# Bucket ranks of the third layer: running totals on VectorE from whole-group counts, in stages

## The reference

```python
Wh = h @ W + b
row, col = (edge_index[0], edge_index[1])
Wr, Wc = Wh[row], Wh[col]
dot = jnp.sum(Wr * Wc, axis=-1)
nr = jnp.sqrt(jnp.sum(Wr * Wr, axis=-1))
nc = jnp.sqrt(jnp.sum(Wc * Wc, axis=-1))
sim = dot / jnp.maximum(nr * nc, EPS)
prop_pos = segment_sum((base * relu(sim))[:, None] * Wc, row, num_segments=n_nodes)
prop_neg = segment_sum((base * -relu(-sim))[:, None] * Wc, row, num_segments=n_nodes)
return scale * (coeff[0] * prop_pos + coeff[1] * prop_neg + coeff[2] * Wh)
```

## Time and profile before

| | |
|---|---|
| median of 3 runs | 9442.85 us (9428.52 to 9460.71) |
| the profiled execution | 9496.65 us, its span 9494.9 us |
| PE busy over the span | 5779.2 us (61%) |
| POOL busy | 5102.6 us (54%) |
| DVE busy | 4579.2 us (48%) |
| ACT busy | 3305.8 us (35%) |
| TensorE's granted clock, mean | 0.748 |

### The profile page before, as it was taken

The page is one execution under the profiler, slowest core; times in us unless marked ns, Lnnn a source line. Parts: engine busy times, 40 slices in busy tenths (PEclk is TensorE's granted clock), DMA queues, the critical chain, the costliest instruction groups (busy, mean ns, idle before and its releaser), DMA issues. The chain is left out here.

```text
span 9494.9 us, 103424 instructions
## 1 busy us (share of the span) xinstructions
PE 5779.2 (61%) x22770; PEld 3507.7 (37%) x22771; DVE 4579.2 (48%) x10542; ACT 3305.8 (35%) x6399; POOL 5102.6 (54%) x5308
## 2 busy tenths in 40 slices
PE   0068788888840777777777524444443444499997
PEld 0034343434320333333333222222222222299997
DVE  2545555555542333333333353444444444477777
ACT  0023333333320333333333311111111111299997
POOL 5666666666656666666666555566655656500000
PEclk9978887878765777777777755555555555599998
DMA  8233333333321333333333211111111111122221
GB/s 325 80 93 111 109 107 110 109 110 106 112 62 49 98 98 103 102 103 103 106 103 104 81 30 55 52 52 53 52 51 51 53 51 53 47 59 59 60 59 52
DMA packets 566846, 800.69 MB, mean 84 GB/s; under 512 B 163210, under 2 KB 307466, under 8 KB 566506
## 3 DMA queue, kind: packets, MB, share of 16 engines
q1 hardware_dynamic: 371944, 482.15, 16.8%
q0 software_dynamic: 172640, 195.75, 9.3%
q10 hardware_dynamic: 22178, 121.99, 3.2%
HBM read 497.93 MB, written 301.41 MB: 84 GB/s over the span
## 5 line engine op out<-in xcount | busy, mean ns | idle before, releaser
L696 POOL DMA_INDIRECT rows_by_src_bucket<-arena,put_idx x1568 | 1532.8, 978 | 1019.2 <-DVE arena L1342 549.3
L625 POOL DMA_INDIRECT G<-h_rows,src_idx x1568 | 1483.2, 946 | 852.7 <-issue 456.2
L625 POOL DMA_INDIRECT G<-in_x,src_idx x1470 | 1395.7, 949 | 808.5 <-issue 432.2
L1172 DVE TENSOR_TENSOR_SCAN xd_t<-same,xd_t,ps_two 128x512 f32<-128x512 bf16 x588 | 749.1, 1274 | 1044.1 <-remote 870.0
L746 PE MATMUL ps_gv<-attr,w_attr 65*128 65x512 f32 x1568 | 1104.1, 842 | 220.4 <-issue 126.3
L749 PE MATMUL ps_gv<-arena,w_src 128*128 128x512 f32 x1568 | 1044.3, 803 | 0.0
L728 PE MATMUL ps_two<-ident,inj 128*128 128x128 f32 x2352 | 445.1, 322 | 938.1 <-DMA inj<-first_edge_rows 648.2
L928 ACT COPY arena<-ps_out 128x512 f32<-128x512 f32 x392 | 230.5, 588 | 2124.7 <-remote 1864.0
L813 PE MATMUL ps_pos<-arena 128*128 128x392 f32 x390 | 316.3, 914 | 1017.1 <-DVE arena L1195 621.9
L1234 DVE TENSOR_SCALAR arena<-ps_gv 128x512 f32<-128x512 f32 x392 | 266.5, 680 | 1228.5 <-remote 607.4
L752 PE MATMUL ps_gv<-xd_t,w_dst 128*128 128x512 f32 x1568 | 773.8, 616 | 3.5 <-issue 3.5
(11 more groups left out here) (226 smaller groups left out, 10251.1 us busy)
## 6 DMA issues: line engine op xcount, KB each, us to landing
inj<-first_edge_rows SPq DMA_DIRECT2D x588, 256.0 KB
running_sums<-arena SPq DMA_DIRECT2D x392, 256.0 KB
same<-same_dst SPq DMA_DIRECT2D x1176, 64.0 KB
rows_by_src_bucket<-zeros ACTq DMA_DIRECT2D x98, 703.5 KB
first_edge_rows<-zeros ACTq DMA_DIRECT2D x56, 896.0 KB
attr<-in_attr_t SPq DMA_DIRECT2D x392, 128.0 KB
G<-h_rows,src_idx POOLq DMA_INDIRECT x1568
rows_by_src_bucket<-arena,put_idx POOLq DMA_INDIRECT x1568
```

The costliest lines, as they stand in the source:

```text
L625: pool.indirect_dma_start(out_, None, table_in, bass.IndirectOffsetOnAxis(ap=index, axis=0)).then_inc(s, 16)
L696: pool.indirect_dma_start(bucket_d, bass.IndirectOffsetOnAxis(ap=put_idx[:, buf, k:k + 1], axis=0), put[:, buf, k], None).then_inc(s_added ...
L1172: v.tensor_tensor_scan(xd_t[:, buf % 2], same[:, buf], ps_inj, xd_t[:, 1 - buf % 2, COLS - 1:COLS], ALU.mult, ALU.add).then_inc(s_scan, 1)
```

## The change

A group's running count no longer passes through the ranks. PE counts the whole group at once (`count_group`: `ones_b` as weights, both halves summed into one of two new buffers `ps_counts`), and DVE adds that to `reached` (`add_counts`), of which there are now 4 buffers. `rank` takes both halves of a group from the same `reached`; the second half gets the marks of the first by one more matmul with `ones_b`. The ranks have two buffers in PSUM (`ps_ranks`), `hot` has 4, `sq` has 2. ACT copies no ranks: only `fill_put` is left. All stages are now written by `pipeline` with lags: on DVE marks 0, carry 1, add 1, place 2; on PE turn and count 0, turn back 1, ranks 1.

```diff
-        hot = tile(2, SLOTS * NT // 2).rearrange("p b c -> p (b c)").bitcast(BF16).rearrange("p (b c) -> p b c", b=2)
+        hot = tile(NB, SLOTS * NT // 2).rearrange("p b c -> p (b c)").bitcast(BF16).rearrange("p (b c) -> p b c", b=NB)
-        reached = tile(2, CB)
-        sq = tile(SLOTS * D)
+        reached = tile(NB, CB)
+        sq = tile(2, SLOTS * D)
+        ps_ranks = ((ps_pos, ps_out), (ps_gv[:, 1, 0], ps_gv[:, 1, 1]))
+        ps_counts = (ps_gv[:, 0, 0], ps_gv[:, 0, 1])
...
-            def place(h, buf):
-                def rank(k):
...
-                turn_inj(2, h, buf)
-                pe.wait_ge(s_hot, done(1, h, buf))
-                rank(0).then_inc(s_below[0], 1)
-                pe.wait_ge(s_scan, done(2, h, buf))
-                pe.wait_ge(s_sq, done(0, h, buf, 1))
-                for j in range(TILES):
-                    mm = pe.transpose(ps_g[:, j * P:(j + 1) * P], turned(xd_t[:, buf % 2], j), ident[:])
-                mm.then_inc(s_wt, 1)
-                rank(1).then_inc(s_below[1], 1)
-            pipeline(pe, (place, 0))
+            def turn_first(h, buf):
+                turn_inj(2, h, buf)
+            def count_group(h, buf):
+                pe.wait_ge(s_hot, done(1, h, buf))
+                pe.wait_ge(s_reached, done(0, h, buf, 1))
+                for k in range(2):
+                    mm = pe.matmul(ps_counts[buf % 2][:, 0:CB], ones_b[:], hot[:, buf, k * CB:(k + 1) * CB],
+                                   start=k == 0, stop=k == 1)
+                mm.then_inc(s_counted, 1)
+            def turn_back(h, buf):
+                pe.wait_ge(s_scan, done(2, h, buf))
+                pe.wait_ge(s_sq, done(0, h, buf, 1))
+                for j in range(TILES):
+                    mm = pe.transpose(ps_g[:, j * P:(j + 1) * P], turned(xd_t[:, buf % 2], j), ident[:])
+                mm.then_inc(s_wt, 1)
+            def rank(h, buf):
+                if at_start(h) and buf == 0:
+                    pe.wait_ge(s_halves, 2)
+                pe.wait_ge(s_reached, done(0, h, buf))
+                for k in range(2):
+                    pe.wait_ge(s_ranked[k], done(0, h, buf, 2))
+                    to = ps_ranks[buf % 2][k][:, 0:CB]
+                    pe.matmul(to, last_row, reached[:, buf], start=True, stop=False)
+                    if k:
+                        pe.matmul(to, ones_b[:], hot[:, buf, 0:CB], start=False, stop=False)
+                    pe.matmul(to, upto[:], hot[:, buf, k * CB:(k + 1) * CB], start=False,
+                              stop=True).then_inc(s_below[k], 1)
+            pipeline(pe, (turn_first, 0), (count_group, 0), (turn_back, 1), (rank, 1))
...
-            def copy_ranks(h, buf):
-                for k, ranks_now in enumerate((ps_pos, ps_out)):
-                    act.wait_ge(s_below[k], done(0, h, buf))
-                    nc.scalar.copy(reached[:, k], ranks_now[:, 0:CB]).then_inc(s_reached[k], 1)
-                    if k == 0:
-                        fill_put(h, buf)
...
-                act.wait_ge(s_norm, done(0, h, buf, 1))
-                nc.scalar.activation(sq, ps_g, ACT.Square).then_inc(s_sq, 1)
+                act.wait_ge(s_norm, done(0, h, buf, 2))
+                nc.scalar.activation(sq[:, buf % 2], ps_g, ACT.Square).then_inc(s_sq, 1)
...
-            pipeline(act, (copy_ranks, 0))
+            pipeline(act, (fill_put, 0))
...
+            def mark_group(h, buf):
+                mark_buckets(1, h, buf)
+            def carry_group(h, buf):
+                carry_dst(2, h, buf)
+            def add_counts(h, buf):
+                dve.wait_ge(s_counted, done(1, h, buf))
+                dve.wait_ge(s_reached, done(0, h, buf))
+                dve.wait_ge(s_below[1], done(0, h, buf, NB - 1))
+                v.tensor_tensor(reached[:, (buf + 1) % NB], reached[:, buf], ps_counts[buf % 2][:, 0:CB],
+                                ALU.add).then_inc(s_reached, 1)
+            def place_group(h, buf):
+                for k in range(2):
+                    dve.wait_ge(s_below[k], done(0, h, buf))
+                    v.tensor_tensor(ranks[:, k], ps_ranks[buf % 2][k][:, 0:CB], hot[:, buf, k * CB:(k + 1) * CB],
+                                    ALU.mult).then_inc(s_ranked[k], 1)
+                    dve.wait_ge(s_ranked[k], done(0, h, buf))
+                    then(v.tensor_reduce(pos[:, k * CLASSES:(k + 1) * CLASSES],
+                                         ranks[:, k].rearrange("p (c t) -> p c t", t=NT), AX.X, ALU.add))
+                put_free(dve, h, buf)
+                v.tensor_scalar(put_idx[:, buf], pos, 0.0, None, ALU.add).then_inc(s_pidx, 1)
+                dve.wait_ge(s_sq, done(0, h, buf))
+                v.tensor_reduce(put[:, buf, :, NORM_AT], by_node(sq[:, buf % 2]), AX.X, ALU.add).then_inc(s_norm, 1)
+            pipeline(dve, (mark_group, 0), (carry_group, 1), (add_counts, 1), (place_group, 2), steps=steps, per=2 * NB)
```

More of the change, by code:

```diff
@@ L343, in gnn @@
         s_ranked = two("ranks_used")
-        s_reached = two("ranks_copied")
+        s_reached = sem("running_counts_ready")
         s_pidx = sem("put_idx_ready")
@@ L764, in count @@
                     for k in range(2):
-                        mm = pe.matmul(ps_pos[:, 0:CB], ones_b[:], hot[:, buf % 2, k * CB:(k + 1) * CB],
+                        mm = pe.matmul(ps_pos[:, 0:CB], ones_b[:], hot[:, buf, k * CB:(k + 1) * CB],
                                        start=at_start(h) and buf + k == 0,
@@ L799, in _ @@
             mm.then_inc(s_bxs, 1)
-            ps_rank = (ps_pos, ps_out)
-            flat_base = base.rearrange("p c t -> p (c t)")
-            def place(h, buf):
-                def rank(k):
[L806 to L818, removed]
+            def turn_first(h, buf):
                 turn_inj(2, h, buf)
+            def count_group(h, buf):
                 pe.wait_ge(s_hot, done(1, h, buf))
-                rank(0).then_inc(s_below[0], 1)
+                pe.wait_ge(s_reached, done(0, h, buf, 1))
[4 more added lines that the diff above has]
+            def turn_back(h, buf):
                 pe.wait_ge(s_scan, done(2, h, buf))
@@ L1190, in mark_buckets @@
                 if rnd == 0:
-                    dve.wait_ge(s_counted, done(0, h, buf, 2))
+                    dve.wait_ge(s_counted, done(0, h, buf, NB))
+                else:
+                    dve.wait_ge(s_below[1], done(0, h, buf, NB))
                 at = ds(h * (NB * SLOTS) + buf * SLOTS, SLOTS)
@@ L1194, in mark_buckets @@
                 for k in range(SLOTS):
-                    mark = v.tensor_scalar(hot[:, buf % 2, k * NT:(k + 1) * NT], lane[:, 0:NT], ids[:, k:k + 1], None,
+                    mark = v.tensor_scalar(hot[:, buf, k * NT:(k + 1) * NT], lane[:, 0:NT], ids[:, k:k + 1], None,
                                            ALU.is_equal)
@@ L1325, in _ @@
                 v.tensor_scalar(bucket_at[0:1, k], ps_out[0:1], float(width), None, ALU.mult).then_inc(s_halves, 1)
[L1327 to L1347, removed]
-                steps.begin(i - 1, 2 * NB)
-                place_group(i)
-            steps.end(TRIPS - 1, 2 * NB)
+            v.tensor_copy(reached[:, 0], base.rearrange("p c t -> p (c t)")).then_inc(s_reached, 1)
+            def mark_group(h, buf):
[8 more added lines that the diff above has]
+                                ALU.add).then_inc(s_reached, 1)
```

2 lines of the change are left out of this document (1 added, 1 removed).

## The result

The changed kernel takes **9345.71 us** (median of 4 runs, 9338.67 to 9360.56), the kernel before 9441.31 us beside it (4 runs, 9428.52 to 9460.71). The ratio is 0.9893, with a 95% interval of 0.9876 to 0.9909: 96 us less, or 1.1%. The profiled execution of the changed kernel took 9360.56 us, its span 9358.7 us.

The account below looks back on a forecast made before the run. POOL's scatters were taken as the floor, with waits for DVE's norms worth at most 535 us. Saving 170 us in 196 groups, less some 8 us longer start, gave -163 us: 9442.85 to 9280 us, range 8900 to 9450.

Parts of the forecast that it names:

- the slow stretches: Scatter loop: stretches while POOL issues unbroken indirect transfers, in which PE's messages arrive 5 to 11 us late.
- ACT's copies are gone: Loop from group to group: 2 x 0.49 us of ACT copies and four hand-overs leave it.
- step 4: Scatter loop outside slow stretches: a group's free period falls from 8.6 to about 6.7 us.
- DVE's add: DVE's queue in the scatter loop: one new 392-wide add, 0.57 us, making 6.5 us a group.
- PE's new matmuls: PE's queue in the scatter loop: 3 more 392-column matmuls, 1.0 to 1.6 us a group.
- The slow stretches stay: Scatter loop: late messages remain; a 6.9 us pause per 3.7 groups gives 12.07 us a group, 170 us less.
- its own signs: Changed profile: loop 2340 to 2400 us, about 55 pauses of 7 us, all released by the norms.
- the 24 us for a group in a slow stretch: Scatter loop: time assumed per group in a slow stretch, from 12 to 13 PE matmuls seen in 20 us.
- the ends of step 5: Group in a slow stretch: 27 us if matmuls go through one by one, 11 if only hand-overs are slow.
- POOL alone: Rival: POOL never waits in the scatter loop, 10.2 us a group, 8916 us in all; chance 0.16.
- No change: Rival: pauses still come each 3 groups, restart takes as long, 9430 to 9450 us; chance 0.17.
- Slower: Rival: PE's matmuls really complete late, 4.9 us more per stalled group, restart about 7 us, 9550 us; chance 0.15.

Follow-up runs that it names:

- u3: The changed kernel with all pipeline lags set to 0, on the chip where the kernel before takes about 9440 us: 9391.3 us, ratio 0.9945.
- u1: The kernel before, unchanged, profiled again on the chip where it takes about 9440 us: 9433.15 us, ratio 0.9997.
- e1: The changed kernel with 4 of each group's 8 scatters left out, on a chip where the kernel before takes 8120 to 8122 us: 7335.66 us.
- e2: The changed kernel with 3 more 392-column matmuls a group, on a chip where the kernel before takes 8120 to 8122 us: 8118.68 us.
- e5: The changed kernel with the marks of 8 slots as one DVE instruction, where the kernel before takes about 9440 us: 9306.43 us, ratio 0.9854.
- e3: The changed kernel with all pipeline lags set to 0, on a chip where the kernel before takes 8120 to 8122 us: 8115.63 us.
- e6: The changed kernel with 6 more 4-column matmuls a group, on a chip where the kernel before takes 8120 to 8122 us: 8116.63 us.
- v1: The changed kernel with 6 more 4-column matmuls a group, run again where the kernel before takes 8120 to 8122 us: 8118.63 us.
- u2: The changed kernel, unchanged, profiled again on the chip where the kernel before takes about 9440 us: 9348.82 us, ratio 0.9907.

## Why the prediction was right, and where its sizes were not

It said 9280 us and -163 us, with a range of 8900 to 9450; it is 9346 us and -96. Faster was right, the mechanism for it in the main too, and the gain was put 1.7 times too high. Two things in it are luck. The range was wide enough to hold an unchanged kernel (9441 us), and it presupposes the slow stretches: on three of the four chips on record there was nothing to be gained. Step by step:

1. *ACT's copies are gone*: as said. u3 shows what that and the new counting give without any stages: 49 us, although its free group is no shorter than before (8.4 to 9.6 us from scan to scan, mostly 9.2, against 8.6). So about half of the gain did not need the shorter free period of step 4. u3's pauses are more and shorter (495 us in 100 pauses, 5.0 us each, against 528 in 74 in u1). With that goes a sooner restart of POOL behind a slow stretch: in the one shown above it is 2.9 us from 6526.20, when the late message comes, to 6529.07, where it was 4.6 in the earlier trace rows.
2. *DVE's add* takes 0.53 us (forecast 0.57) and its queue 6.2 us, by e1 (forecast 6.5).
3. *PE's new matmuls* cost nothing that can be seen: e2 has three more again and loses nothing on chip B.
4. *The free group*: 6.7 us forecast, 6.25 measured, and e1 shows it over a whole loop, bound by DVE. Right.
5. *The slow stretches stay*: right, and the long pauses, 60 before, became 47 (the forecast counted about 65 and 55). **Here is the term that was mis-sized.** It took every cycle as alike: one pause of 6.9 us to each 3.7 groups, 1.9 us a group. There is one pause to 2.6 groups, of 6.0 us on average, 2.3 us a group. Part of that was to be seen beforehand: the sum starts from 65 pauses, 3.0 groups apart, read off a single cycle, while the earlier trace rows has 84 waits and the trace 79 pauses, 2.5 groups apart. By its own signs the forecast missed here too: the loop takes 2433 us, not 2340 to 2400, there are 75 pauses, not 55, and 20 waits are released by ACT's `put` and not by the norms. The 28 short pauses were not reckoned with: 86 us, 39 more than before. And the 24 us for a group in a slow stretch counted PE's matmuls alone; what the trace after shows there is DVE's queue slowed as well, up to 9.4 us for the marks alone, in a place where the kernel before hardly ever made marks. e5, which has one row where there were eight, gets back 42 us of the 67 that were missing (26 of them seen in the profiled loops), though perhaps in part through its shorter free group.

The choice between the ends of step 5 (27 or 11 us a group) was to rest on whether PE's instructions go through one by one. That was not settled: the three kernels made for it met chip B. The ends of rows on PE can't settle it either. The Trainium skill (Perfetto Trace Analysis, Tensor Engine Instruction) says that these ends are computed, so how late PE itself was in a slow stretch is not seen. What the traces do show speaks against the 27-us end, without being a test of it. In a slow stretch PE's rows start close together: four L826 stand within 1.13 us, where 1.6 us each would spread them over 5. PE's register rows are never slow either. So "12 to 13 matmuls in 20 us" is an average of bursts and waits, not a rate that is seen. DVE's marks are another matter: they do start one by one, 1.4 us apart.

The rivals. *POOL alone* (0.16) is what chip B shows in e2, e3, e6 and v1, and not what happened on chip A. *No change* needed pauses each 3 groups and an unchanged restart; the pauses do often come each 3 groups (24 scatters stand between them in 47 of 76 unbroken sequences), but many are short. *Slower* did not come. Its piece of truth is the restart, which it put at 7 us: in u2 POOL starts 5.7 us behind the scan that ends a slow stretch (6520.94 to 6526.65), not 3.3, since the staged DVE makes scan and sum before it places the group for which POOL waits.

TensorE's clock is 0.66 in the loop, where about 0.6 was said, and 0.58 before.

The reading of the profile went wrong at one more place, which a single chip could not have shown. "I take it as the rule of this kernel" was said of the slow stretches. They came on one of the four chips on record, or with what surrounded it, and on none of the others.

## What to carry to other kernels

When a stage pauses at regular intervals while every engine has room, look at what is slow in the pause and count everything that will now fall into it: stages with lags move instructions into the bad stretch, and here the register rows of an engine's sequencer were slow there as well as its messages. One wide instruction with broadcast operands in place of eight narrow ones gave 42 us here, on an engine that was no bound. And run the kernel before on more than one chip before a stall is explained by the program: the same program took 14% less time on the others, and the change worth 1.1% here was, by all that ran there, worth nothing.

## What was not expected of the hardware

- The same program takes 9440 us on one chip and 8120 to 8122 on three others. The last loop, without POOL's indirect transfers, takes the same (1221 us in u3 and e3); the stages with them don't (the scatter loop of that kernel 2477 and 2003 us).
- On the slower chip, unbroken scatters at 1.28 us apiece go along with messages of PE that arrive 8 to 10.5 us late, with DVE instructions 1.4 us apart that are 0.2 us apart otherwise, and with register rows of DVE's and SP's sequencers of up to 1.5 us (PE's and ACT's stay under 0.1). On the faster ones none of this is seen in 2000 us of the same scatters (e2, e3). Why the chips differ was not found, and that the scatters are the cause was not tested on the slower one.
- A GpSimd fill of 1024 columns with a wait for its own end, in front of each group's scatters, costs 1.8 us a group, of which the fill is 0.96.
